# Rotary swap by small transfers, and a new split of the second norm and the rotary between VectorE and GpSimd

## The reference

```python
xn = _layernorm(x)                                   # the "second norm"
q, k, v = xn @ wq, xn @ wk, xn @ wv                  # one head, 128 wide
def fractional_rope(z):                              # for q and k
    rot, skip = split(z, 2)                          # 64 + 64
    even, odd = split(rot, 2)                        # 32 + 32
    return concat(even * cos - odd * sin, even * sin + odd * cos, skip)
s = (q @ k.T) / 128 - 1e30 * mask                    # causal
x_attn = softmax(s) @ v @ wo
h = silu((xn @ w1.T) * s1) * ((xn @ w2.T) * s2)      # the "gates"
h = gelu((h @ h1.T) * sh1); h = gelu((h @ h2.T) * sh2)
out = x + x_attn + (h @ w3.T) * s3
```

## Time and profile before

| | us |
|---|---|
| median of three runs | 266.39 (266.19 to 266.41) |
| the profiled execution | 266.38 |
| its span, first to last instruction | 264.6 |
| layer 0 with the last chunk of its output | 0 to 84 |
| second norm, projections, rotary | 84 to 102 |
| attention and gates | 102 to 203 |
| the network's two hidden layers and the output | 203 to 264.6 |

### The profile page before, as it was taken

One profiled execution on the slowest core, in us unless ns is written; L12 is line 12 of the kernel. 1 busy time (PEld: TensorE's weight loads), 2 busy tenths in 40 slices (PEclk: granted clock), 3 DMA queues, 4 the chain that ended last, 5 costly groups with the idle time before them and its releaser, 6 DMA issues.

```text
span 264.6 us, 5188 instructions
## 1 busy us (share of the span) xinstructions
PE 248.1 (94%) x1664; PEld 160.1 (61%) x1668; DVE 211.4 (80%) x717; ACT 191.5 (72%) x473; POOL 114.3 (43%) x146
## 2 busy tenths in 40 slices
PE   7789899999967799999999999999999999999992
PEld 2258454557625348686777778777876444444482
DVE  5967799999996899898899986986643797666684
ACT  1689897866563798787667899999841997777730
POOL 9989200000000568988765697787972000000000
PEclk9999999999999999999999999999999999999999
DMA  7710000000000832200000000000000000000014
GB/s 196 214 31 2 0 1 2 1 0 2 2 0 4 339 139 57 105 1 1 0 2 0 2 0 2 2 0 0 2 0 2 0 0 1 4 0 0 0 29 136
DMA packets 8303, 8.50 MB, mean 32 GB/s; under 512 B 1745, under 2 KB 7378, under 8 KB 7762
## 3 DMA queue, kind: packets, MB, share of 16 engines
q1 hardware_dynamic: 7442, 7.65, 9.0%
q10 hardware_dynamic: 832, 0.49, 0.7%
HBM read 7.09 MB, written 1.05 MB: 31 GB/s over the span
## 4 chain that ended last, share of the span: by engine, by line
PE 46%; DVE 33%; POOL 6%; ACT 6%; issue 4%; DMA 2%; DVEq 0%; SPq 0%; POOLq 0%; ACTq 0%
PE PS L909 10%; PE PS L910 10%; PE PS L882 7%; PE PS L859 7%; PE PS L872 4%; DVE arena L1692 3%; POOL arena L1430 3%; POOL arena L1431 3%; DVE arena L1679 2%; DVE arena L1711 2%; DVE arena L1720 2%; DVE mxb L1938 2%; DMA x<-L_attn_x 2%; DVE arena L1697 2%; DVE arena L1924 1%
## 5 line engine op out<-in xcount | busy, mean ns | idle before, releaser
L909 PE MATMUL PS<-arena 128*128 128x512 f16 x128 | 48.5, 379 | 0.0
L910 PE MATMUL PS<-arena 128*128 128x512 f16 x128 | 48.5, 379 | 0.0
L1996 DVE TENSOR_TENSOR arena<-arena 128x512 f32<-128x512 f32 x32 | 22.2, 692 | 13.0 <-ACT arena L1358 13.0
L859 PE MATMUL PS<-arena 128*128 128x512 f32 (+3 forms) x80 | 31.9, 530 | 0.3 <-ACT arena L1327 0.3
L1357 ACT ACTIVATE arena<-PS,arena 128x512 f32<-128x512 f32 x32 | 22.9, 717 | 9.0 <-PE PS L910 9.0
L1430 POOL TENSOR_TENSOR arena<-arena 128x256 f32<-128x256 f32 x32 | 21.6, 675 | 15.5 <-DVE arena L1930 13.0
L1438 POOL CAST arena<-arena 128x512 f16<-128x512 f32 x2 | 1.3, 636 | 60.3 <-ACT x L1220 60.3
L1327 ACT ACTIVATE arena<-PS,lnt 128x512 f32<-128x512 f32 (+3 forms) x40 | 24.8, 628 | 2.9 <-DVE lnt L1945 2.8
L1431 POOL TENSOR_TENSOR arena<-arena,small 128x256 f16<-128x256 f32 (+1 forms) x36 | 23.8, 662 | 2.8
L1358 ACT ACTIVATE arena<-PS,arena 128x512 f16<-128x512 f32 x32 | 22.9, 714 | 0.0
L1938 DVE TENSOR_REDUCE mxb<-PS 128x1 f32<-128x512 f32 (+3 forms) x40 | 22.1, 601 | 0.0
(11 more groups left out here) (284 smaller groups left out, 629.7 us busy)
## 6 DMA issues: line engine op xcount, KB each, us to landing
arena<-h_T SPq DMA_DIRECT2D x2, 1024.0 KB, 5.7
x<-L_attn_x SPq DMA_DIRECT2D x4, 256.0 KB, 4.7
arena<-cos SPq DMA_DIRECT2D x1, 1024.0 KB, 4.7
arena<-sin SPq DMA_DIRECT2D x1, 1024.0 KB, 6.9
arena<-w_T SPq DMA_DIRECT2D x3, 256.0 KB, 3.0
out<-arena SPq DMA_DIRECT2D x2, 256.0 KB, 2.3
con<-shape_constants ACTq DMA_DIRECT2D x1, 192.0 KB, 3.5
out<-arena SPq DMA_DIRECT2D x1, 192.0 KB, 2.1
```

What stands on the lines that cost most here:

```text
L859: i = mm(PS[:, k, 0:cnt * P], qT1[:, t * P:(t + 1) * P], kT1[:, c * P:(c + cnt) * P], start=True, stop=not last)
L909: mm(bank(b), wH[:, k, m * P:(m + 1) * P], sH[:, k, cols], start=(k == 0), stop=False)
L910: i = mm(bank(b), wL[:, k, m * P:(m + 1) * P], sL[:, k, cols], start=False, stop=(k == HT4 - 1))
L1996: v.tensor_tensor(RP[m], FP[m], high, ALU.subtract).then_inc(rest_ready, 1)
```

## The change

The projection with `wswap` is gone. VectorE multiplies the one projection by both tables; the sine product is then moved between the two groups of 32 partitions by four DMAs per chunk into `SWAPPED` (the sine table has its signs exchanged for that). One more DMA moves the skipped half of k, which ScalarE now copies together with q's in one instruction. Both rotary sums are made by GpSimd. Of each chunk's norm tiles one goes from VectorE to GpSimd. `TURN` has four buffers. The rotary products of chunk 0 stand inside the norm, ahead of chunks 2 and 3. The tables are loaded in layer 0, both hidden weights behind the last rotary sum. GpSimd also takes the two casts of the mask constants from ScalarE. TensorE's order and banks follow.

```diff
@@ buffers
-        TURN = [hBf[:, T * c:T * c + 2 * BANK].rearrange("p (k t) -> p k t", k=2) for c in range(2)]
-        xd = hBf[:, T + 2 * BANK:T + 3 * BANK]
+        TURN = [hBf[:, 2 * BANK * c:2 * BANK * (c + 1)].rearrange("p (k t) -> p k t", k=2) for c in range(4)]
+        SWAPPED = [hBf[:, 2 * T + BANK * c:2 * T + BANK * (c + 1)] for c in range(4)]
+        xd = Pr[1][:, T - BANK:T]
+        SWAPS_IN = 16 * 6
@@ sync
-            sp.wait_ge(x1_ready, 2)
+            sp.wait_ge(lanes_done, 4)
             for i, n in enumerate(("cos", "sin")):
                 sp.dma_start((cosT, sinT)[i], a[n]).then_inc(tab_in, 16)
-            sp.wait_ge(x1_ready, 4)
+            for c in range(4):
+                cols = slice(c * BANK, (c + 1) * BANK)
+                sp.wait_ge(rope_dve, 2 * c + 1)
+                for p0 in range(0, P, ROT):
+                    for p in (p0, p0 + ROT // 2):
+                        q = 2 * p0 + ROT // 2 - p
+                        sp.dma_start(SWAPPED[c][q:q + ROT // 2, :], TURN[c][p:p + ROT // 2, 1, :]).then_inc(chunk_in[c], 16)
+                sp.wait_ge(skip_act, c + 1)
+                sp.dma_start(kT1[0:ROT, cols], qT1[ROT:P, cols]).then_inc(chunk_in[c], 16)
+            sp.wait_ge(turned_pool, 8)
             sp.dma_start(h1S, a["h1_T"]).then_inc(h_in[0], 16)
-            sp.wait_ge(turned_dve, 4)
-            sp.wait_ge(turned_pool, 4)
             sp.dma_start(h2S, a["h2_T"]).then_inc(h_in[1], 16)
@@ tensor
-                mm(bank(b + 2), wturn, xc, start=True, stop=True).then_inc(turn_done, 1)
-                mm(bank(b + 3), wswap, xc, start=True, stop=True).then_inc(turn_done, 1)
+                mm(bank(TURN_BANK[c]), wturn, xT[:, c * BANK:(c + 1) * BANK], start=True, stop=True).then_inc(turn_done, 1)
...
             normed(0)
-            for c in range(4): ...
+            turned(0)
+            normed(1)
+            skipped(0)
+            pe.wait_ge(x1_ready, 4)
+            turned(1)
+            skipped(1)
+            normed(2)
             values(0)
+            turned(2)
+            normed(3)
+            skipped(2)
+            turned(3)
+            skipped(3)
@@ scores
-                    pe.wait_ge(skip_act, t // 2 + 2)
-                    pe.wait_ge(turned_dve, t // 4 + 1)
-                    pe.wait_ge(turned_pool, t // 4 + 1)
+                    pe.wait_ge(skip_act, t // 4 + 1)
+                    pe.wait_ge(turned_pool, t // 2 + 2)
@@ scalar
+            def skipped(c):
+                act.wait_ge(skip_done, c + 1)
+                f(qT1[:, c * BANK:(c + 1) * BANK], bank(SKIP_BANK[c]), ACT.Copy).then_inc(skip_act, 1)
-                f(qT1[0:ROT, cols], PS[0:ROT, b + 1, :], ACT.Copy).then_inc(skip_act, 1)
-                f(kT1[0:ROT, cols], PS[ROT:P, b + 1, :], ACT.Copy).then_inc(skip_act, 1)
@@ gpsimd
-            pool.wait_ge(x1_ready, 4)
-            (w1H, w1L, w2H, w2L, four sums for k, four low inputs)
+            def second_normed(c):
+                n = 4 * c + 3
+                pool.wait_ge(x1_ready, max(c + 1, 2))
+                pool.wait_ge(shift_ready, c + 1)
+                nc.gpsimd.tensor_scalar(xn[:, n, :], x[:, n, :], mv[:, n, 0:1], lnt[:, 1, n:n + 1], ALU.subtract, ALU.mult).then_inc(xn_ready, 1)
+            def rotated(c):
+                cols = slice(c * BANK, (c + 1) * BANK)
+                pool.wait_ge(rope_dve, 2 * c + 2)
+                pool.wait_ge(chunk_in[c], SWAPS_IN)
+                for k, (to, h) in enumerate(((kT1, slice(ROT, P)), (qT1, slice(0, ROT)))):
+                    tt(to[ROT:P, cols], TURN[c][h, 0, :], SWAPPED[c][h, :], ALU.add).then_inc(turned_pool, 1)
+                    pool.wait_ge(turned_pool, 2 * c + k + 1)
...
+            rotated(0)
+            low_weights(w2L, w2T)
+            low_input(0)
+            rotated(1)
+            rotated(2)
+            low_input(1)
+            rotated(3)
+            low_input(2)
+            low_input(3)
@@ vector
-                for n in range(4 * c + 2, 4 * c + 4):
-                    v.tensor_scalar(xn[:, n, :], ...)
+                n = 4 * c + 2
+                v.tensor_scalar(xn[:, n, :], ...)
             for c in range(4):
+                if c == 2:
+                    dve.wait_ge(tab_in, 32)
+                    rotary(0, 1)
+                if c == 3:
+                    rotary(0, 0)
                 shifts(c)
                 normed(c)
...
-            (per chunk: cosine product, sine product, sum for q)
+            for c in range(1, 4):
+                rotary(c, 1)
+                rotary(c, 0)
```

More of the change, by code:

```diff
@@ L122, in take @@
             return arena[:, at[0] - n:at[0]]
-        wturn, wswap, wskip, wvT2, wo, WVO, s3 = (take(P) for _ in range(7))
+        wturn, wskip, wvT2, wo, WVO, s3 = (take(P) for _ in range(6))
         w1T, w2T, w3T = (take(HID) for _ in range(3))
@@ L265, in program @@
         fits_flag = sb("fits_flag", [1, 1], I32)
-        x_in = [sem(f"x_in{c}") for c in range(4)]
+        chunk_in = [sem(f"chunk_in{c}") for c in range(4)]
         early_in, eta_in, moe_in, late_in = sem("early_in"), sem("eta_in"), sem("moe_in"), sem("late_in")
@@ L777, in normed @@
                 pe.wait_ge(xn2_act, 2 * c + 2)
[L778 removed]
+                pe.wait_ge(xn2_dve, c + 1)
+                pe.wait_ge(xn_ready, NT + c + 1)
                 if c >= 2:
@@ L1249, in _ @@
             transposed(0)
+            normed(1)
             first_block(3)
-            normed(1)
             deviations(2)
+            transposed(1)
             normed(2)
-            transposed(1)
+            skipped(0)
             deviations(3)
+            transposed(2)
             normed(3)
-            transposed(2)
+            skipped(1)
+            transposed(3)
             f(small[:, 38:39], lnt[:, 0, 12:13], ACT.Tanh)
-            for c in range(4):
-                b = 4 * ((c + 1) % 2)
-                cols = slice(c * BANK, (c + 1) * BANK)
-                act.wait_ge(skip_done, c + 1)
-                f(qT1[0:ROT, cols], PS[0:ROT, b + 1, :], ACT.Copy).then_inc(skip_act, 1)
-                f(kT1[0:ROT, cols], PS[ROT:P, b + 1, :], ACT.Copy).then_inc(skip_act, 1)
-                if c == 0:
-                    transposed(3)
-                if c == 2:
-                    act.wait_ge(xt2_act, 1)
-                    high(0)
-                    f(ident_b, ident, ACT.Copy).then_inc(mask_act, 1)
-                    f(causal_b, con[:, C_CAUSAL:C_CAUSAL + P], ACT.Copy).then_inc(mask_act, 1)
+            skipped(2)
+            act.wait_ge(xt2_act, 1)
+            high(0)
+            skipped(3)
             act.wait_ge(xt2_act, 4)
@@ L1443, in _ @@
+            def rotated(c):
                 cols = slice(c * BANK, (c + 1) * BANK)
                 pool.wait_ge(rope_dve, 2 * c + 2)
-                tt(kT1[ROT:P, cols], TURN[c % 2][ROT:P, 0, :], TURN[c % 2][ROT:P, 1, :], ALU.add).then_inc(turned_pool, 1)
-            for c in range(4):
+                pool.wait_ge(chunk_in[c], SWAPS_IN)
+                for k, (to, h) in enumerate(((kT1, slice(ROT, P)), (qT1, slice(0, ROT)))):
+                    tt(to[ROT:P, cols], TURN[c][h, 0, :], SWAPPED[c][h, :], ALU.add).then_inc(turned_pool, 1)
+                    pool.wait_ge(turned_pool, 2 * c + k + 1)
@@ new lines, in _ @@
+            second_normed(0)
+            nc.gpsimd.tensor_copy(ident_b, ident).then_inc(mask_set, 1)
+            nc.gpsimd.tensor_copy(causal_b, con[:, C_CAUSAL:C_CAUSAL + P]).then_inc(mask_set, 1)
+            pool.wait_ge(small_in, 16 * 12)
+            high_weights(w1H, w1T)
+            second_normed(1)
+            low_weights(w1L, w1T)
+            second_normed(2)
+            high_weights(w2H, w2T)
+            second_normed(3)
+            pool.wait_ge(xn_ready, NT + 4)
+            rotated(0)
```

102 lines of the change are left out of this document (43 added, 59 removed).

## The result

The changed kernel takes 267.85 us (median of 4 runs, 267.4 to 268.59), against 266.4 us of the kernel before on the same chip (4 runs, 266.19 to 266.5). The ratio is 1.0054 with a 95% interval of 1.004 to 1.0068: slower by about 0.5%. The prediction was 265.5 us, so it had the sign wrong.

A forecast was written before the change was run, and what follows sets the result against it. TensorE and VectorE were taken to bound the kernel together. The front gains 4.0 us, but GpSimd's low parts come 2.6 us late against 3.5 us of slack, leaving 0.9 us: 265.5 us, own range 264.9 to 266.1, 8-in-10 range 263.2 to 268.0.

The forecast's parts named there:

- D: Lateness of gate 0's low part on GpSimd, 115.5 us in place of 112.94: 2.6 us; net gain is 3.5 - D.
- the shift by one constant: Behind gate 7 on VectorE and TensorE: all the rest moves by the same 0.9 us earlier.
- The front, 4.0 us: Up to the first scores: TensorE starts them at 97.7 us in place of 101.70, VectorE ready at about 97.6 us.
- the early products: Chunk 0's two rotary products inside VectorE's norm: fill two square-root waits of 0.36 us each, saving 0.7 us.
- The landing, 94.5 us: Chunk 0's transfers on SP: fifth issued at 92.0 us, landing between 94.2 and 95.1 us, taken as 94.5.
- The sum on GpSimd, 1.14 us: Each rotary sum on GpSimd takes 1.14 us without VectorE's neighbouring sum; eight with seams take 9.9 us.
- The slack at gate 7, 3.5 us: On VectorE before the change: its buffer was free at 115.81 us, gate 7 started at 119.36 us.
- the forecast gain, 0.9 us: At gate 7 and for the whole kernel: gate 7 starts at 118.4 us, 0.9 us earlier than before.
- rival A: GpSimd's sums stay at 1.75 us, D 7.5 us, kernel 270.4 us; decides from D of 3.5 us; chance 0.22.
- the pinch is once only: At gates 6 and 7: no later buffer waits, as low parts follow every 1.5 us, two gates every 4 us.
- The moved tables and weights: Loads of tables and hidden weights, moved by whole stages: costed at nothing, as the DMA engines are almost unused beside attention.
- that rule, 267.4 us: GpSimd at twice VectorE's time: a sum of 1.38 us, D 4.5, kernel 1.0 us slower at 267.4 us.

The follow-up runs named there:

- experiment 4: Changed kernel with eight buffers for the gates' inputs in place of six, GpSimd's work unmoved: 262.96 us, ratio 0.9869 to the kernel before.
- 1: Changed kernel with two of the input's four low parts moved on GpSimd behind the gates of tiles 5 and 8: 263.65 us, ratio 0.9898.
- experiment 9: Repeat of the changed kernel with eight buffers of gate inputs in place of six: 262.72 us, ratio 0.9874 to the kernel before.
- experiment 8: Fourth norm tile of each chunk back on VectorE, in the changed kernel with eight buffers and separate skipped-half semaphore, 263.97 us; with eight buffers alone, 264.93 us.
- experiment 2: Changed kernel with 18 and 8 unused products on ones in TensorE's idle times ahead of gates 8 and 9: 267.3 us, ratio 1.0036.
- experiment 7's first kernel: Changed kernel with eight buffers of gate inputs and a separate semaphore for the skipped half's transfer: 263.84 us, ratio 0.9894 to the kernel before.
- experiment 7's second kernel: Changed kernel with eight buffers and separate skipped-half semaphore, but chunk 0's rotary products behind the norm on VectorE: 267.09 us, ratio 1.0016.

## Why the prediction was wrong

Its structure held up to gate 7. VectorE waits at gates 6 and 7, GpSimd's low parts end the wait, the wait goes when a buffer is free (experiment 4) or when the low parts come in time (1), and what the front gained beyond the slack is lost. What failed is the size of D, GpSimd's delay, and behind gate 7 the shift by one constant. Point by point:

- **The front, 4.0 us.** Measured 3.5 us (98.24 us), and 3.8 us in the trace without the dip in layer 0 (97.89 us, experiment 9). TensorE alone would have been ready at about 97.7 us, as forecast; the last 0.15 us are the chain of product, transfers and sums, which I had ready by 97.0 us. VectorE's time in the norm does count, as said: with the norm tile given back TensorE's last projection is 0.7 us later (experiment 8). But more of what the front gained hangs on the start of the transfers: giving back the norm tile costs 1.6 us at the first scores, giving back the early products, which I costed at 0.7 us of VectorE's time, 2.6 us (100.45 us).
- **The landing, 94.5 us.** Wrong by 1.0 us (95.53), of which 0.4 us is the dip in layer 0 and 0.6 us the issue of the transfers, one every 0.62 us in place of 0.47 us: the fifth is issued 2.5 us behind the first and not 1.9 us. The landing itself, 2.3 us for the 128 KB, was at the lower end of what I took, and from its issue to the first sum it was 2.48 us where I had 2.5.
- **The sum on GpSimd, 1.14 us.** Measured 1.27 us. Eight sums with their seams took 10.8 us in place of 9.9, and the low parts 0.1 us less than I took. I had two rows that differed and chose the wrong one. L1465, a product of two f32 operands, took 1275 ns; the difference that took 1.16 us has xH as its second operand, which is f16. That it is the operand and not the operation, this row of the kernel after tells, a difference of two f32 operands:

```profile
L1515 POOL TENSOR_TENSOR arena<-arena 128x512 f32<-128x512 f32 x11 | 14.0, 1272 | 0.9
```

The sums read two f32 operands, and so do as these. What I took off the old sums for VectorE's neighbour was a little too much: from 1.27 us, the overlaps of 0.57 and 0.64 us cost 0.44 and 0.51 us.
- **The step that failed: D = 2.6 us.** The stream behind the first sum took 117.25 - 95.53 = 21.7 us in place of 21.0, and began 1.0 us late: D = 4.3 us, and 4.0 us in the trace without the dip (116.90 us, experiment 9). The slack at gate 7, 3.5 us, was right: 3.5 - 4.3 = -0.8 us against 0.89 us measured. All of the forecast gain, 0.9 us, was this one difference of two numbers, and two terms mis-sized by 0.6 and 0.7 us turned it round, with the dip on top. In the prediction's own terms it passed the point from which rival A decides (D of 3.5 us), though not by the sum alone: 2.6 + 0.7 = 3.3 us.
- **A step that failed too: one constant behind gate 7.** I had everything behind gate 7 shifted by gate 7's own shift. Gate 7 is 0.9 us late, gate 10 1.4 us, TensorE's last product 1.7 us. A term that wasn't there is TensorE's clock: I forecast that TensorE would idle for 3 us ahead of gate 10 and counted its idle time only, but a clock of 0.57 for 4 us came with it, 0.6 us at gate 10 (experiment 2). With the clock at 1.00 gate 10 is 0.8 us late, about as gate 7, and still the last product is 1.6 us late. So the other part is lost behind gate 10. GpSimd, late as it is, runs without a pause up to 142.7 us, and VectorE's casts last longer beside it: the five from 126 to 141 us take 1.93 us before and 2.79 us in experiment 2's trace, 0.86 us more, just what TensorE loses there from gate 10 to gate 19 (0.80 to 1.66 us late). In the kernel after they take 2.22 us, 0.29 us more, and it loses 0.26 us. So "the pinch is once only" was too simple; the agreement in size is read from the traces, and no run tests it by itself. Experiment 2's kernel is still slower than before by 0.36% [0.22 to 0.5], so the clock alone does not explain the sign.
- **Nothing else cost much.** The moved tables and weights, the transfers of chunks 1 to 3: nobody waits for them in the trace, and experiment 4, which leaves all of them in place, gains 3.4 us on the kernel before (3.7 us in its repeat).

The Trainium skill (GPSIMD Engine Reference, "Engine selection") puts GpSimd at about twice VectorE's time for two inputs. Measured was 1.27 / 0.69 = 1.84 times, nearer to it than the 1.65 times that I took, and the time that the prediction worked out by that rule, 267.4 us, is the nearest of those that it worked out. In part this is luck: the rule's sum of 1.38 us is longer than the 1.27 us measured, which makes up for the transfers' late start, and the loss behind gate 7 is in neither.

## What to carry to other kernels

When work is put ahead of other work on an engine that looks half idle, the time that counts is the slack of the first buffer that its later work gives back. If the gain is a difference of two such times, take each operand's type into account before reading a duration off a similar row, and look for another buffer first: two buffers were worth 4.9 us here, moving two low parts 4.2 us, a faster start of the sums 0.7 us. An idle stretch that a change creates on TensorE may bring a low clock behind it, so look at both; but what a neighbour's wait takes back again (0.6 us at gate 10, 0.07 us at the last product) only the rows further on tell. And where a row names a releaser, see whether that instruction ends there: in experiment 8 it did not.

## What the runs showed of the hardware

- SP issues a transfer from buffer to buffer of 32 or 64 partitions in 0.59 us, the next 0.62 us after it; loads from outer memory took 0.43 and 0.47 us. In experiment 8 four of them took 3.30 and 3.67 us in place of 2.46. They land 2.0 us (64 KB) and 2.3 us (128 KB) after issue.
- On GpSimd 64 partitions cost as much as 128: 1266 ns for 64x512 (sums) and 1275 and 1272 ns for 128x512 (products, differences), all of two f32 operands; a difference with f16 for the second operand took 1.16 us.
- A cast of 128x256 on VectorE took from 0.29 to 1.18 us. In experiment 7's first kernel 7 of the 20 casts behind 119 us took 0.29 us; the other 13 all began while GpSimd was at an instruction and ended 0.14 or 0.15 us behind its end, however long that was (in the kernel before and the kernel after, 0.14 to 0.16 us). So a cast that starts earlier beside a busy GpSimd does not end earlier. The Trainium skill (SBUF — State Buffer, "Who interferes with whom") says of casts in VectorE's 2-port mode that whoever issues first has the shared ports for its whole instruction and the other is blocked; the rows agree, though which mode these casts ran in no run shows. It took back what the clock gave in experiment 2, and stands at the place where experiment 7's first kernel loses to experiment 4's.
- TensorE's clock was 0.58 and 0.57 in the 4 us behind two stretches in which it was busy for 1.2 of 4 us, and 1.00 in the same place when products on ones filled them. In 8 of the 14 traces it fell to 0.50 to 0.57 for some stretch of 2 us between 80 and 88 us; ahead of that TensorE had done the same work in the kernel after, which has the dip, as in the kernel before, which has not. In experiment 7's second kernel it fell behind 2.68 us of idle time in the same way (0.64 and 0.50).
